# A relational graph layer on one core: gathered edge rows in plain f32 against weighted one-hot tables

## The chip, the cores and the metric

The kernel runs on one core of one Trainium2 chip. Its time is the device time of one execution, in microseconds (us). The kernel before took 3181.22 us, the median of three executions (3174.54 to 3181.66).

The engines are TensorE (PE; its weight loads have a row of their own, PEld), VectorE (DVE), ScalarE (ACT), GpSimd (POOL) and SyncE (SP), which issues most transfers. Each runs its own instructions in order and waits for the others at semaphores.

## The reference

`x` is 12500 nodes by 256 channels; there are 200000 edges, sorted by destination, each with a source, one of 8 types and a weight. Cut to what matters:

```
xn  = layernorm(x)
msg = xn[src] * edge_weight
h   = segment_sum(msg, type*N + dst) / max(count, 1)      # mean over (type, dst)
gnn = einsum('rnc,rco->no', h, weight) + xn @ root + bias
mix = linear attention of xn (8 heads, elu+1 features, one global k-v sum) @ wo + bo
x   = x + gnn + mix
x   = x + mixture_of_experts(layernorm(x))                # router, 6 experts of 3 layers, best 2
```

## The kernel before

**First stage (phase A).** The products `xn @ weight[r]` are formed for all nodes and 8 types and written to a table `y_tab` of 100000 rows of 256 floats in device memory. A table `etab` holds for each edge the row of `y_tab` that it needs, its destination, and its coefficient (weight over count). An edge's message is then one row of `y_tab` times one coefficient. This stage is the same in both kernels.

**Second stage (phase C)** works through 25 groups of up to 512 nodes (4 tiles of 128; the last group has 2). For each tile of nodes, 17 tiles of 128 edges are gathered: GpSimd issues one indirect DMA for each tile of edges into `ring` (L1159). A group's 68 tiles of edges come in 12 portions of 6, 6 and 5, and `ring` holds 6 portions. The sum over destinations is a matmul: the weights are a table `sel` (edge by node, 1 where the edge ends in the node), the moving operand is the 128 x 256 tile of rows, and the result is added in the PSUM accumulator `acc` of that tile of nodes.

**Precision.** Every large product is made from fp32r operands split in two: a high part, and a low part that is the rest. For the edges the table is exact, so two matmuls do: `sel` x `row_hi` and `sel` x `row_lo`. ScalarE makes `row_hi = fp32r(row * coefficient)` (L1216), VectorE makes `row_lo = row * coefficient - row_hi` (L1394) and the tables, one instruction for a portion (L1388), from a ramp that lies in PSUM. `sel` and `row_hi` have two buffers, `row_lo` six.

**Order within a loop pass i** (24 passes i = 0 to 23, then a last short one for the last 2 tiles). While the dense layers of group i run, the portions of group i+1 are put between them on TensorE. TensorE's order in a pass is: `queries` and `root` of group i+1; `turn` (8 transposes of the normalised group i, which wait for VectorE's layer norm, `xn_c`); portions 0 and 1 (`aggregate`, L1709); router and first layer of expert 0; portion 2; then for each expert e the second layer of e, a portion if `BEHIND_H2` names one, the first layer of e+1, the portion that `AHEAD_W3` names, and the third layer of e; at the end `close_sum`, 8 products in plain f32 into the same accumulators (L1718). All split products are recorded at one helper line, L1655. The results of the dense layers go to five PSUM banks in turn; ScalarE and VectorE split each first or second layer's result (L1230, L1231, then L1473), and VectorE adds each third layer's result to `y` (L1540). ScalarE and VectorE have the edge work written in between these: `high` on ScalarE, `one_hot` and `low_rows` on VectorE.

Group 0's portions run ahead of the loop, together with 36 key and value products (L1655 with `xk`, L1810), in the stretch that is called the middle here.

Of the kernel before, what the change touches and what calls it, by code (L numbers as in the profile page):

```python
# [16 lines left out]
NT = P  # L17
# [19 lines left out]
SLOTS, BUFS = 6, 2  # L37
# [4 lines left out]
BEHIND_H2 = {2: 5, 3: 7, 4: 9}  # L42

# [9 lines left out]
def gps_layer(nc, x, src, dst, etype, ew, g_w, g_root, g_b, wq, bq, wk, bk, wv, bv, wo, bo,  # L53
# [21 lines left out]
    with whole:  # L75
# [800 lines left out]
        with pc:  # L876
# [47 lines left out]
            gate_t = rq[0:8, 1, :]  # L924
            with ExitStack() as px:
                ring = sbuf(px, "ring", [P, SLOTS, PT, C])
# [93 lines left out]
            hi_ready, lo_ready, portion_used = (sem(n) for n in ("hi_ready", "lo_ready", "portion_used"))  # L1020
# [23 lines left out]

            def between(e):
                return BEHIND_H2.get(e, AHEAD_W3.get(e, PARTS))
# [148 lines left out]
            def _(act):  # L1195
# [13 lines left out]
                def high(n, p, first=0, end=PT):  # L1209

                    if first == 0:
                        act.wait_ge(tab_in[n % 2], 16 * SUB * (n // 2 + 1))
                        act.wait_ge(rows_in[p % SLOTS], 16 * gathers(n, p))
                        act.wait_ge(portion_used, portions_before(n, p) - BUFS + 1)
                    for q, (t, k) in list(enumerate(tiles_of_portion(p)))[first:end]:
                        last = act.activation(row_hi[:, p % BUFS, q, :], ring[:, p % SLOTS, q, :],  # L1216
                                              ACT.Copy, scale=tab[:, n % 2, t, k, 2:3])
                    if end == PT:
                        last.then_inc(hi_ready, 1)

                def iteration(i, plan):
# [18 lines left out]
                    if more:  # L1240
                        high(i + 1, 2)
# [4 lines left out]
                    if more:  # L1246
                        high(i + 1, 3)
                    act.wait_ge(d_ready, i + 1)
                    act.activation(ex[:, 0:T, :], lg[:, 0:T, :], ACT.Exp).then_inc(ex_ready, 1)
                    for e in range(EXPERTS):  # L1250
                        for m in range(KC):
                            hidden("h2", e, m)
                            if more and e in BEHIND_H2 and AHEAD_W3[e] < parts(i + 1):
                                high(i + 1, AHEAD_W3[e], 3 * m, 3 * m + 3)
# [8 lines left out]
                        if more and between(e + 1) < parts(i + 1):  # L1263
                            high(i + 1, between(e + 1))
                    if more:
                        if i + 2 < SUPER:
                            for p in range(2):
                                high(i + 2, p)
# [16 lines left out]
                for p in range(PARTS):  # L1285
                    if p < LATER:
                        for j in range(SUB):
                            key_parts(SUB * p + j)
                            if p and j < 2:
                                high(0, p - 1, 3 * j, 3 * j + 3)  # L1290
                    else:
                        if p == LATER:
                            high(0, p - 1)
                        high(0, p)
# [13 lines left out]
                for p in range(2):  # L1308
                    high(1, p)
# [5 lines left out]
            def _(dve):  # L1315
# [29 lines left out]
                dve.tensor_copy(ramp[:, 0:P], iota_w[:, :])  # L1345
                dve.drain()
# [53 lines left out]
                def prepare(n, p):  # L1400
                    one_hot(n, p)
                    low_rows(n, p)
# [479 lines left out]
```

## Time and profile before

| | |
|---|---|
| timed, median of 3 | 3181.22 us |
| profiled execution, span | 3900.9 us |
| TensorE busy, of the span | 3132.7 us |
| VectorE busy | 2360.3 us |
| ScalarE busy | 2004.5 us |
| GpSimd busy | 1638.6 us |
| mean granted TensorE clock | 0.894 of 2.4 GHz |

The profiled execution is one execution with the profiler on; its span is 3900.9 us, 720 us above the timed median. Both numbers are needed to read this case: durations and orders come from the profiled one, the result is a timed one. A matmul is written with two records, one of PEld and one of PE; a matmul in plain f32 has two of each. Because matmuls overlap, the distance from one start to the next, and not the duration, is what one costs in a row of them.

### The profile page before, as it was taken

How to read it: one execution, taken by the hardware profiler on the slowest of the kernel's cores; microseconds unless marked ns; L12 is line 12 of the kernel's file. 1: busy time of each engine (PE TensorE's matmuls, PEld its weight loads, DVE VectorE, ACT ScalarE, POOL GpSimd, SP SyncE). 2: the span in 40 equal slices, each digit the busy share in tenths (PEclk: the TensorE clock that was granted, in tenths of full speed). 3: DMA queues.
4: the chain of work that ended last, by engine and by line, in shares of the span. 5: the costliest groups of instructions: out<-in, count | busy, mean ns of one | idle time of the engine just before them, and what ended most of it. 6: DMA issues, size and time to landing. Idle time of an engine off the chain costs nothing.

```text
span 3900.9 us, 48061 instructions
## 1 busy us (share of the span) xinstructions
PE 3132.7 (80%) x16807; PEld 2709.1 (69%) x16808; DVE 2360.3 (61%) x5405; ACT 2004.5 (51%) x3996; POOL 1638.6 (42%) x1696
## 2 busy tenths in 40 slices
PE   6999999766878778777777777787787778787788
PEld 5888887656767767666666667676676667677677
DVE  4497552246666667566666656666565666666675
ACT  3555555334555555454555555555555455545564
POOL 0000000145555555554555555554545455555540
PEclk9999999888888888888889888888888889898899
DMA  6665555543233333233323333233323333233320
GB/s 242 250 259 196 210 210 212 224 144 112 84 93 95 99 96 94 82 94 91 90 77 96 95 92 89 85 97 89 92 83 91 90 93 91 79 97 93 100 67 11
DMA packets 179841, 456.72 MB, mean 117 GB/s; under 512 B 46604, under 2 KB 104918, under 8 KB 159405
## 3 DMA queue, kind: packets, MB, share of 16 engines
q0 software_dynamic: 80352, 219.14, 19.5%
q1 hardware_dynamic: 97074, 232.64, 16.5%
q8 instruction: 134, 2.20, 0.2%
q10 hardware_dynamic: 2172, 1.85, 0.1%
q14 instruction: 109, 0.89, 0.1%
HBM read 296.01 MB, written 158.29 MB: 116 GB/s over the span
## 4 chain that ended last, share of the span: by engine, by line
PE 41%; another core or an unknown queue 12%; DVE 10%; ACT 10%; issue 7%; DVEq 1%; DMA 0%; SPq 0%; ACTq 0%
PE bank L1655 27%; PE acc L1709 7%; DVE row_lo L1394 4%; ACT row_hi L1216 4%; ACT bank L1231 3%; ACT h_hi L1230 2%; PE acc L1718 1%; PE bank L1793 1%; PE bank L1682 1%; PE bank L1691 1%; PE acc L1655 1%; DVE y L1540 1%; DVE h_lo L1473 1%; DVE sel L1388 1%
## 5 line engine op out<-in xcount | busy, mean ns | idle before, releaser
L1159 POOL DMA_INDIRECT ring<-y_tab,tab x1666 | 1624.1, 975 | 1401.6 <-PE acc L1709 869.9
L1230 ACT ACTIVATE h_hi<-bank,bias_t 128x512 fp32r<-128x512 f32 (+1 forms) x600 | 408.9, 682 | 1078.1 <-remote 565.1
L1709 PE MATMUL acc<-row_hi,sel 128*128 128x256 f32 x1666 | 501.6, 329 | 446.5 <-DVE row_lo L1394 255.5
L1709 PEld LDWEIGHTS acc<-row_hi,sel 128*128 128x128 f32 x1666 | 369.9, 222 | 508.3 <-DVE row_lo L1394 291.1
L1216 ACT ACTIVATE row_hi<-ring,tab 128x256 fp32r<-128x256 f32 x1666 | 704.1, 510 | 31.4 <-PE acc L1709 19.4
L1394 DVE SCALAR_TENSOR_TENSOR row_lo<-ring,tab,row_hi 128x256 fp32r<-128x256 f32 x1666 | 685.1, 479 | 48.9 <-ACT row_hi L1216 34.4
L1473 DVE TENSOR_TENSOR h_lo<-bank,h_hi 128x512 fp32r<-128x512 f32 (+1 forms) x600 | 392.6, 676 | 447.2 <-ACT bank L1231 360.5
L790 PE MATMUL yb<-wr_hi,xhl 128*128 128x512 f32 x1568 | 510.9, 398 | 31.5 <-ACT yst L351 25.4
L1655 PE MATMUL bank<-ew_hi,h_hi 128*128 128x256 f32 x1176 | 384.2, 327 | 179.0 <-DVE h_lo L1473 177.7
L1709 PE MATMUL acc<-row_lo,sel 128*128 128x256 f32 x1666 | 480.9, 315 | 13.4 <-issue 13.2
L1540 DVE SCALAR_TENSOR_TENSOR y<-bank,gate,y 128x256 f32<-128x256 f32 x490 | 213.0, 479 | 349.7 <-PE bank L1655 227.7
L1655 PEld LDWEIGHTS bank<-ew_hi,h_hi 128*128 128x128 f32 x1176 | 268.7, 229 | 198.9 <-DVE h_lo L1473 196.3
L351 ACT ACTIVATE yst<-yb 128x512 f32<-128x512 f32 x392 | 230.5, 595 | 321.3 <-PE yb L790 283.6
L1231 ACT ACTIVATE bank<-bank,bias_t 128x512 f32<-128x512 f32 (+1 forms) x600 | 392.1, 654 | 0.0
L1709 PEld LDWEIGHTS acc<-row_lo,sel 128*128 128x128 f32 x1666 | 374.3, 225 | 11.3 <-issue 8.2
L1655 PE MATMUL bank<-ew_lo,h_hi 128*128 128x256 f32 x1176 | 371.2, 316 | 0.0
L790 PEld LDWEIGHTS yb<-wr_hi,xhl 128*128 128x128 f32 x1568 | 296.2, 189 | 104.6 <-ACT yst L351 26.3
L1655 PE MATMUL bank<-ew_hi,h_lo 128*128 128x256 f32 x1176 | 367.4, 312 | 0.0
L790 PE MATMUL yb<-wr_lo,xhl 128*128 128x512 f32 x784 | 311.5, 397 | 0.0
L1388 DVE TENSOR_TENSOR sel<-ramp,rel_w 128x768 fp32r<-128x768 f32 (+1 forms) x294 | 265.6, 903 | 6.4 <-issue 4.9
L1655 PEld LDWEIGHTS bank<-ew_lo,h_hi 128*128 128x128 f32 x1176 | 267.6, 228 | 0.1
L1655 PEld LDWEIGHTS bank<-ew_hi,h_lo 128*128 128x128 f32 x1176 | 264.9, 225 | 0.0
(272 smaller groups left out, 5219.7 us busy)
## 6 DMA issues: line engine op xcount, KB each, us to landing
y_tab<-yst SPq DMA_DIRECT2D x97, 1024.0 KB, 3.9
ring<-y_tab,tab POOLq DMA_INDIRECT x1666
xt_tab<-xhl SPq DMA_DIRECT2D x25, 1024.0 KB, 3.9
xc<-xt_tab SPq DMA_DIRECT2D x25, 1024.0 KB
x<-x_tab SPq DMA_DIRECT2D x49, 256.0 KB
xs<-in_x SPq DMA_DIRECT2D x24, 512.0 KB, 6.0
x_tab<-xs SPq DMA_DIRECT2D x24, 512.0 KB, 5.0
out<-y SPq DMA_DIRECT2D x24, 512.0 KB
```

What stands on the lines that cost most here:

```text
L351: act.activation(yst[:, h, 2 * b:2 * b + 2, :], yb[(YB * u + b) % 3][:, :].rearrange("p (r n) -> p r n", r=2), ACT.Copy).then_inc(y_ev, 1)
L790: last = pe.matmul(out_ap, a, b, start=(i == 0), stop=(i == len(parts) - 1))
L1159: pool.indirect_dma_start(out=out_ap, out_offset=None, in_=y_tab[:, :], in_offset=bass.IndirectOffsetOnAxis(ap=idx_ap, axis=0)).then_inc(s ...
L1216: last = act.activation(row_hi[:, p % BUFS, q, :], ring[:, p % SLOTS, q, :], ACT.Copy, scale=tab[:, n % 2, t, k, 2:3])
L1230: act.activation(dest[:, m, 0:W], b[:, 0:W], ACT.Relu, bias=bias)
L1231: act.activation(b[:, 0:W], b[:, 0:W], ACT.Relu, bias=bias).then_inc(h_set, 1)
L1388: dve.tensor_tensor(sel[:, p % BUFS, 0:size, :], ramp[:, 0:P].unsqueeze(1).to_broadcast([P, size, NT]), rel_w[:, n % 2, t, k:k + size].uns ...
L1394: last = dve.scalar_tensor_tensor(out=row_lo[:, p % SLOTS, q, :], in0=ring[:, p % SLOTS, q, :], scalar=tab[:, n % 2, t, k, 2:3], in1=row_h ...
L1473: gone(dve.tensor_tensor(lo_[:, m, 0:W], bank[plan[kind, (e, m)][0]][:, 0:W], hi[:, m, 0:W].bitcast(F32), ALU.subtract))
L1540: last = dve.scalar_tensor_tensor(out=y[:, t, :], in0=b[:, (t % 2) * C:(t % 2 + 1) * C], scalar=gate[:, t, e:e + 1], in1=(y if e else x1)[ ...
L1655: last = pe.matmul(out_ap, a, b, start=(begin and i == 0), stop=(not more and i == len(parts) - 1), skip_group_check=more)
L1709: last = pe.matmul(sums(t), sel[:, p % BUFS, q, :], half, start=False, stop=False, skip_group_check=True)
```

## The change

ScalarE no longer makes `row_hi`, VectorE no longer makes `row_lo`, and both buffers are gone. VectorE writes, for each tile of edges, a table that holds the edge's coefficient in place of the 1: one tensor_scalar of 128 x 128, (ramp is_equal destination) times coefficient, from SBUF to SBUF. TensorE multiplies this table with the gathered rows as they arrived, both in plain f32: one matmul as written for each tile of edges in place of two. TensorE waits for the rows and for the tables itself. `sel` has four buffers instead of two and is prepared further ahead. The PSUM bank that held the ramp becomes a sixth bank for the dense layers. Portion 0 stands ahead of the transposes instead of behind them. The gathers, the number of tiles and all dense work are the same.

```diff
-SLOTS, BUFS = 6, 2
+SLOTS, BUFS = 6, 4
+READY_AT = {0: (5,), 1: (6,), 2: (7, 8), 3: (9, 10), 4: (11,)}
...
-            row_lo = sbuf(pc, "row_lo", [P, SLOTS, PT, C], F32R)
-            row_hi = sbuf(pc, "row_hi", [P, BUFS, PT, C], F32R)
-            sel = sbuf(pc, "sel", [P, BUFS, PT, NT], F32R)
+            sel = sbuf(pc, "sel", [P, BUFS, PT, NT])
...
-            NBANK = 5
+            NBANK = 6
-            ramp = psum(pc, "ramp")
...
-                def high(n, p, first=0, end=PT):
-                    if first == 0:
-                        act.wait_ge(tab_in[n % 2], 16 * SUB * (n // 2 + 1))
-                        act.wait_ge(rows_in[p % SLOTS], 16 * gathers(n, p))
-                        act.wait_ge(portion_used, portions_before(n, p) - BUFS + 1)
-                    for q, (t, k) in list(enumerate(tiles_of_portion(p)))[first:end]:
-                        last = act.activation(row_hi[:, p % BUFS, q, :], ring[:, p % SLOTS, q, :],
-                                              ACT.Copy, scale=tab[:, n % 2, t, k, 2:3])
...
-                def one_hot(n, p):
+                def prepare(n, p):
+                    if p >= parts(n):
+                        return
                     dve.wait_ge(portion_used, portions_before(n, p) - BUFS + 1)
-                    (t, k), size = tiles_of_portion(p)[0], len(tiles_of_portion(p))
-                    dve.tensor_tensor(sel[:, p % BUFS, 0:size, :], ramp[:, 0:P].unsqueeze(1).to_broadcast([P, size, NT]),
-                                      rel_w[:, n % 2, t, k:k + size].unsqueeze(2).to_broadcast([P, size, NT]), ALU.is_equal)
-                def low_rows(n, p):
-                    dve.wait_ge(hi_ready, PARTS * n + p + 1)
                     for q, (t, k) in enumerate(tiles_of_portion(p)):
-                        last = dve.scalar_tensor_tensor(out=row_lo[:, p % SLOTS, q, :], in0=ring[:, p % SLOTS, q, :],
-                                                        scalar=tab[:, n % 2, t, k, 2:3],
-                                                        in1=row_hi[:, p % BUFS, q, :].bitcast(F32),
-                                                        op0=ALU.mult, op1=ALU.subtract)
-                    last.then_inc(lo_ready, 1)
+                        last = dve.tensor_scalar(sel[:, p % BUFS, q, :], iota_w[:, :], rel_w[:, n % 2, t, k:k + 1],
+                                                 tab[:, n % 2, t, k, 2:3], ALU.is_equal, ALU.mult)
+                    last.then_inc(sel_ready, 1)
...
                 def aggregate(n, p):
-                    pe.wait_ge(lo_ready, PARTS * n + p + 1)
+                    pe.wait_ge(sel_ready, PARTS * n + p + 1)
+                    pe.wait_ge(rows_in[p % SLOTS], 16 * gathers(n, p))
                     for q, (t, k) in enumerate(tiles_of_portion(p)):
-                        for half in (row_hi[:, p % BUFS, q, :], row_lo[:, p % SLOTS, q, :]):
-                            last = pe.matmul(sums(t), sel[:, p % BUFS, q, :], half, start=False, stop=False,
-                                             skip_group_check=True)
+                        last = pe.matmul(sums(t), sel[:, p % BUFS, q, :], ring[:, p % SLOTS, q, :], start=False, stop=False,
+                                         skip_group_check=True)
...
                         root(i, plan)
+                        aggregate(i + 1, 0)
                     turn(i, plan)
                     if more:
-                        aggregate(i + 1, 0)
                         aggregate(i + 1, 1)
```

TensorE at the start of a loop pass, before: behind `root` (the first two rows, into `acc`) come the transposes of the layer-normed group, and only then portions 0 and 1. The last two rows stand twelve times in turn, for the high and the low rows of 12 tiles of edges; the router's first products follow.

```order
L1655 MATMUL acc<-wqr_lo,xc 128x256
L1655 MATMUL acc<-wqr_hi,xc 128x256
L1701 MATMUL bank<-ident,xn_c 128x128 x8
L1709 MATMUL acc<-row_hi,sel 128x256
L1709 MATMUL acc<-row_lo,sel 128x256
```

The same place in the changed kernel, to the router's first products:

```order
L1592 MATMUL acc<-wqr_lo,xc 128x256
L1592 MATMUL acc<-wqr_hi,xc 128x256
L1648 MATMUL acc<-ring,sel 128x256 x6
L1638 MATMUL bank<-ident,xn_c 128x128 x8
L1648 MATMUL acc<-ring,sel 128x256 x6
L1592 MATMUL bank<-ft_hi,rw_hi 128x512
```

Portion 0 moved ahead of the transposes, portion 1 stayed behind them, and each counts 6 matmuls as written instead of 12.

VectorE from the second layer of expert 3 to its third layer, before. The first `h_lo` row belongs to the second layer's first half; `sel` and `row_lo` rows are edge work for the next portions.

```order
L1473 TENSOR_TENSOR h_lo<-bank,h_hi 128x512
L1388 TENSOR_TENSOR sel<-ramp,rel_w 128x640
L1473 TENSOR_TENSOR h_lo<-bank,h_hi 128x512
L1394 SCALAR_TENSOR_TENSOR row_lo<-ring,tab,row_hi 128x256 x5
L1473 TENSOR_TENSOR h_lo<-bank,h_hi 128x512 x2
L1388 TENSOR_TENSOR sel<-ramp,rel_w 128x768
L1540 SCALAR_TENSOR_TENSOR y<-bank,gate,y 128x256 x2
L1394 SCALAR_TENSOR_TENSOR row_lo<-ring,tab,row_hi 128x256 x6
L1540 SCALAR_TENSOR_TENSOR y<-bank,gate,y 128x256 x2
```

The same place in the changed kernel, with the rows of expert 4's layers behind it:

```order
L1421 TENSOR_TENSOR h_lo<-bank,h_hi 128x512 x4
L1350 TENSOR_SCALAR sel<-iota_w,rel_w,tab 128x128 x12
L1480 SCALAR_TENSOR_TENSOR y<-bank,gate,y 128x256 x4
L1341 TENSOR_SCALAR rel_w<-tab 128x17 x4
L1421 TENSOR_TENSOR h_lo<-bank,h_hi 128x512 x4
```

The edge work that stood between the splits of the dense layers is gone; what is left of it is one run of 12 short instructions ahead of the additions to `y`.

## Rows read from the trace of the kernel before

**Rows 1.** The page: span, and busy time, share and instructions of each engine.

```profile
span 3900.9 us, 48061 instructions
PE 3132.7 (80%) x16807; PEld 2709.1 (69%) x16808; DVE 2360.3 (61%) x5405; ACT 2004.5 (51%) x3996; POOL 1638.6 (42%) x1696
```

**Rows 2.** Busy time by stretch: one pass, A, middle, 23 loop passes, rest.

```profile
core 0: us, PE busy (x) PEld busy (x) DVE busy (x) ACT busy (x) POOL busy (x), PEclk, DMA share, GB/s
1186.36:1305.05 118.69, 94.09 (x535) 82.80 (x534) 77.56 (x187) 63.94 (x129) 65.20 (x67) 0.88 0.31 93
0.00:744.00 744.00, 701.19 (x3238) 572.12 (x3239) 400.85 (x735) 391.62 (x725) 14.23 (x29) 0.98 0.60 222
744.00:933.80 189.80, 122.24 (x587) 99.19 (x586) 95.05 (x188) 68.68 (x158) 98.75 (x95) 0.80 0.49 163
933.80:3776.00 2842.20, 2197.16 (x12283) 1937.71 (x12282) 1787.18 (x4279) 1476.43 (x2974) 1525.58 (x1572) 0.87 0.31 91
3776.00:3901.00 125.00, 112.08 (x704) 100.07 (x702) 77.17 (x204) 67.77 (x139) 0.00 (x0) 0.95 0.04 14
```

**Rows 3.** Waits by who waited for whom, whole span: us in total, times, longest.

```profile
ACT h_hi L1230 <- remote: 565.1, 79, 11.1
...
PE acc L1709 <- DVE row_lo L1394: 255.5, 81, 8.9
...
PE acc L1709 <- issue: 203.1, 71, 7.1
...
PE bank L1655 <- DVE h_lo L1473: 179.6, 36, 10.5
```

**Rows 4.** Timeline of one late hand-over: start, us, instruction, [idle before <-releaser].

```profile
1208.78 0.39 PE L1655 MATMUL bank<-ft_hi,ew_lo 128*128 128x512 f32 x1
...
1218.54 0.69 ACT L1230 ACTIVATE h_hi<-bank,bias_t 128x512 fp32r<-128x512 f32 x1 [8.95 <-remote]
```

**Rows 5.** Timeline of TensorE: matmuls in a row, by kind.

```profile
1183.10 3.62 PE L1718 MATMUL acc<-kw_sb,qf 128*128 128x256 f32 x16
...
1192.20 1.07 PE L1701 MATMUL bank<-ident,xn_c 128*128 128x128 f32 x8
...
1195.78 0.28 PE L1709 MATMUL acc<-row_hi,sel 128*128 128x256 f32 x1
1195.90 0.28 PE L1709 MATMUL acc<-row_lo,sel 128*128 128x256 f32 x1
...
1198.64 0.39 PE L1655 MATMUL bank<-ft_lo,ew_hi 128*128 128x512 f32 x1
1198.87 0.39 PE L1655 MATMUL bank<-ft_hi,ew_lo 128*128 128x512 f32 x1
```

**Rows 6.** Groups by line and shape, whole span: busy, mean ns, idle before.

```profile
L1718 PE MATMUL acc<-kw_sb,qf 128*128 128x256 f32 x400 | 91.2, 379 | 2.4 <-issue 2.4
```

**Rows 7.** Groups of one pass, VectorE and ScalarE: busy us, mean ns, idle before.

```profile
L1394 DVE SCALAR_TENSOR_TENSOR row_lo<-ring,tab,row_hi 128x256 fp32r<-128x256 f32 x68 | 27.9, 480 | 2.4 <-ACT row_hi L1216 1.7 <-issue 0.5
...
L1388 DVE TENSOR_TENSOR sel<-ramp,rel_w 128x768 fp32r<-128x768 f32 x8 | 7.6, 947 | 0.1
L1388 DVE TENSOR_TENSOR sel<-ramp,rel_w 128x640 fp32r<-128x640 f32 x4 | 3.3, 816 | 0.0
...
L1216 ACT ACTIVATE row_hi<-ring,tab 128x256 fp32r<-128x256 f32 x68 | 28.7, 510 | 0.1
```

**Rows 8.** Timeline of VectorE's tensor_scalar in runs of four, 128x128 and 128x256.

```profile
107.97 0.86 DVE L480 TENSOR_SCALAR diag<-ident,vmm 128x128 f32<-128x128 f32 x4
...
1190.67 1.38 DVE L1494 TENSOR_SCALAR xn_c<-x,mv_c,rstd_c 128x256 f32<-128x256 f32 x4
```

**Rows 9.** Timeline: two waits of TensorE for VectorE.

```profile
1180.16 0.39 PE L1655 MATMUL bank<-ew_hi,h_hi 128*128 128x256 f32 x1 [1.67 <-DVE h_lo L1473]
...
1196.97 0.47 PE L1655 MATMUL bank<-ft_hi,rw_hi 128*128 128x512 f32 x1 [0.80 <-DVE ft_lo L1503]
```

**Rows 10.** Timeline of GpSimd: one of a row of gathers.

```profile
1204.01 0.94 POOL L1159 DMA_INDIRECT ring<-y_tab,tab  x1 [0.30 <-issue]
```

More of the change, by code:

```diff
@@ L1042, in portions_before @@
                 return PARTS * n + p + SLOTS
-            def between(e):
-                return BEHIND_H2.get(e, AHEAD_W3.get(e, PARTS))
             def tiles_of_portion(p):
@@ L1262, in iteration @@
                             gone(act.activation(gate_t[:, 0:W], take(i, plan, "gt", 0)[0:8, 0:W], ACT.Copy))
[L1263 to L1268, printed above, removed]
                 act.dma_start(wo_sb[:, :, :], wo.rearrange("(k p) n -> p k n", p=P)).then_inc(small_c, 16)
@@ L1463, in iteration, with low @@
                     more = plan is LOOP
-                    def low(kind, e, table=None):
+                    def low(kind, e):
                         if e == EXPERTS:
@@ L1469, in low @@
                         for m in range(KC):
-                            if m and table is not None:
-                                one_hot(i + 1, table)
                             dve.wait_ge(h_set, nth_hidden(i, kind, e, m) + 1)
@@ L1487, in iteration @@
                     last.then_inc(var_c, 1)
-                    if more:
-                        one_hot(i + 1, 1)
                     dve.wait_ge(std_c, i + 1)
@@ L1509, in iteration @@
                     if more:
-                        prepare(i + 1, 3)
+                        prepare(i + 1, 4)
                     for e in range(EXPERTS):
-                        second = AHEAD_W3[e] if more and e in BEHIND_H2 and AHEAD_W3[e] < parts(i + 1) else None
-                        low("h2", e, second)
-                        if second is not None:
-                            low_rows(i + 1, second)
+                        low("h2", e)
                         if e == 0:
@@ L1524, in iteration @@
                             attention(i, plan)
-                        if more and e == EXPERTS - 1:
-                            if i + 2 < SUPER:
-                                prepare(i + 2, 0)
-                        coming = between(e + 1) if more and between(e + 1) < parts(i + 1) else None
-                        if coming is not None:
-                            one_hot(i + 1, coming)
+                        for p in READY_AT.get(e, ()) if more else ():
+                            prepare(i + 1, p)
+                        if e == EXPERTS - 1 and i + 2 < SUPER:
+                            prepare(i + 2, 0)
+                            prepare(i + 2, 1)
                         if e == 0:
@@ L1591, in _ @@
                             if p and j == 0:
-                                one_hot(0, p - 1)
-                            if p and j == 2:
-                                low_rows(0, p - 1)
+                                prepare(0, p - 1)
                     else:
@@ L1763, in iteration @@
                         hidden("h2", e)
-                        if more and BEHIND_H2.get(e, PARTS) < parts(i + 1):
+                        if more and e in BEHIND_H2:
                             aggregate(i + 1, BEHIND_H2[e])
@@ L1768, in iteration @@
                             denominators(i, plan)
-                        if more and AHEAD_W3[e] < parts(i + 1):
+                        if more:
                             aggregate(i + 1, AHEAD_W3[e])
```

36 lines of the change are left out of this document (7 added, 29 removed).

## The prediction

> **What bounds the kernel now.** I read the page first for its shares, then the stretches, then TensorE's timeline for what a matmul costs, then the waits.
>
> The page gives TensorE the largest share, 80% [rows 1], and the stretches show that the edges matter in one part only: phase A is the same in both kernels; the middle (190 us) holds the edges of group 0; 23 loop passes take 2842.2 us, 123.6 each; the last 125 us hold pass 23 and the short pass [rows 2]. So the argument is about a loop pass.
>
> The profiled execution is 720 us longer than the timed median of 3181 us, and that has to be placed before any sum. In phase A TensorE is busy for 701 of 744 us, so little of the excess can lie there. In the loop there are waits that no work explains. In [rows 4] TensorE has recorded the first layers up to 1209.2, but ScalarE, which had nothing to do but take a bank, starts at 1218.54 and is released by nothing that the profile names. Such waits sum to 565 us on ScalarE, and TensorE stands still for 203 us more with no releaser [rows 3]: 768 us together, about the 720. I take them for a burden of the profiled execution. That is an inference, since no timed run has a trace.
>
> What a timed pass takes follows from the median. Outside the loop and its tail are 933.8 us profiled; I take 29 us off for waits of the same kind and slow clock in the middle (granted 0.80 [rows 2]), and get 905. The short last pass is about 38 of the last 125 us. Pass 23 prepares only 34 tiles of edges, so it has 8 us less of matmuls. So 24 passes b give 3181 = 905 + 24b - 8 + 38, **b = 93.6 us**.
>
> What TensorE alone needs comes from distances between starts at full clock (2.4 GHz) [rows 5]: a split product of 512 columns costs 0.231 (1198.64 to 1198.87; in other places 0.227 to 0.234), one of 256 columns 0.119 (1195.78 to 1195.90), and a record of a plain f32 product of 256 columns 0.216: 16 of them in 3.62 us, the last lasting 0.379 [rows 6], so (3.62 - 0.38)/15. The code gives the counts of a pass, 534, which the stretch of one pass bears out with 535 records [rows 2]. 162 of 512 columns make 37.4 us. 304 of 256 columns make 36.2, of which the edges' 136 are 16.2. 24 plain f32 records make 5.2. 44 small ones at 0.11 (8 transposes in 1.07 us, the last lasting 0.28) make 4.8. That is **83.6 us**. A timed pass then has 93.6 - 83.6 = 10 us in which TensorE waits: TensorE is nearly the bound now, and the rest are hand-overs from VectorE and ScalarE (row_lo, h_lo) [rows 3].
>
> **The change, part by part, for one loop pass.**
>
> *Fewer but dearer matmuls.* 68 tiles of edges had two matmuls at 0.119, 0.238 us a tile. They get one as written, in plain f32 with the same 128 x 256 shape as `close_sum`, whose 200 products as written show 400 records [rows 6]. So a tile costs two records at 0.216, 0.432 us. The difference is 0.194 x 68 = **+13.2 us** on TensorE. Nothing can hide work on the engine that is itself the bound. TensorE's own work becomes 83.6 - 16.2 + 29.4 = 96.8 us: above the whole timed pass of today. The weight load of f32 lasts less than the 0.216 and overlaps, as it does in `close_sum`. I see no cheaper end for this price, since the row is of the same shape and kind.
>
> *ScalarE.* 68 `row_hi` of 28.7 us go [rows 7]. ScalarE falls from 63.9 to 35 us. This is worth something only through TensorE's waits, since ScalarE takes the dense results out of the banks and the edge work stood between them.
>
> *VectorE.* 27.9 + 7.6 + 3.3 = 38.8 us go [rows 7]. 68 tensor_scalars of 128 x 128 come. Four `diag` of that shape take 0.86 us, 0.215 each; the upper bound is the 128 x 256 form with two column operands, 1.38/4 = 0.345 [rows 8]; below the first I see no reason to go. I take the first, which has the shape: 14.6 us (at most 23.5). VectorE falls from 77.6 to 53 us (at most 62). Both lie beside TensorE's 96.8. Where the tables are made, in one run ahead of the additions to `y`, 12 of them take 2.6 us (at most 4.1); TensorE meanwhile has two portions (5.2 us) and a first layer (2.8 us) ahead of the third layer, and the six banks leave room. So this costs nothing; without that cover it would be 2 us for each of three experts, +6.
>
> *The new waits of TensorE* are for rows and tables. GpSimd starts a gather every 1.24 us (0.94 and 0.30 idle [rows 10]), 68 of them in 84.6 us a pass, 12 us under TensorE's work, with six portions of slack in `ring`. The tables are made four portions ahead. Both are ready.
>
> *Portion 0 ahead of the transposes.* From the end of `close_sum` the layer norm takes about 5.8 us to `xn_c`, and `queries` (2.8) and `root` (2.9) just cover it today. Portion 0 adds 2.6 us of cover. Behind the transposes portion 1 now lasts 2.6 us, where two portions lasted 2.9, so the 0.80 us wait for `ft_lo` stays [rows 9].
>
> *What remains of the 10 us of waiting.* The waits for `row_lo` go by construction. Those for `h_lo` shrink: between the end of a second layer and its use TensorE has 5.4 us of work and needs two steps of ScalarE and one of VectorE, some 2.1 us, no longer held up by edge work. I keep the 0.80 and the 1.67 us behind expert 5 [rows 9], where no first layer follows: **2.5 us**. The pass is 96.8 + 2.5 = 99.3 us, 5.7 more than 93.6.
>
> *The middle.* TensorE has +13 us for 68 tiles. But this stretch is bound by VectorE's hand-overs, and in each of nine portions 3.3 us of VectorE (`sel` 0.9, six `row_lo` of 0.4) become 1.2, -18. Net -5.
>
> *Sum.* 23 x 5.7 = 131. Pass 23 has 34 tiles: +6.6 of work, less 7.5 of waits, -1. Middle -5. 3181 + 125 = 3306; I say **3310**.
>
> Against the profiled span the same sum holds for the work (+13.2 a pass); what the span itself will be depends on the unexplained waits, which I can't forecast: if they stay, about 3900.9 + 125.
>
> **Two rules of the skill.** GpSimd's gathers start every 1.24 us beside VectorE's work today [rows 10]. The Trainium skill (SBUF — State Buffer, "SBUF: two separate sides") says that while VectorE runs an instruction that reads through both its ports, GpSimd can't write descriptors, and f32 tensor_scalar from SBUF to SBUF would be one. An estimate by it adds at most the 14.6 us of the new tables to 84.6, 99.2, just level with the 99.3 of a pass, so the sum would stand; with the upper bound of the tables it would be 108 and GpSimd the bound, which is the third rival. No row here shows a gather held up by such an instruction. The second is about the price of a matmul. The rows show 0.231 and 0.119 us at full clock [rows 5]. The Trainium skill (TensorE: Matmul & The Clock Gate, "Back-to-back issue gap") gives columns/2.4 GHz + 2.5 ns, so 0.216 and 0.109: the plain f32 record agrees with it, the split products don't. What that would do is the second rival.
>
> **Rivals.**
>
> *Nothing is given back.* The 10 us of waiting might be of the dense layers' own hand-overs and stay. Then every pass takes the full +13.2: 3181 + 23 x 13.2 + 6.6 + 13 = 3504. For it speaks that `h_lo` is among the waits [rows 3]; against it that `row_lo` is the larger one, and that a longer run of edge matmuls covers the others. Chance 0.10.
>
> *TensorE has more room than it seems* (the other side). If the fp32r products run in timed executions at 0.216 and 0.109, the place is every product of every stage. TensorE's need today is then 83.6 - 162 x 0.015 - 304 x 0.010 = 78.1, after the change 96.8 - 162 x 0.015 - 168 x 0.010 = 92.7; phase A with its 2724 products of 512 columns (98 tiles x 24 and 62 x 6) is 48 us shorter, so b = 95.6. A pass becomes 95.2, and the whole 3181 - 9 - 8 - 5 = 3159. It decides as soon as a timed pass of today exceeds TensorE's new need plus its waits. Against it: in the same pass the plain f32 records stand 0.216 apart [rows 5], so the profiler doesn't keep TensorE from that distance, and what makes the split products longer is theirs. Chance 0.08.
>
> *GpSimd becomes the bound.* If the new tensor_scalars hold up the gathers by more than 14.7 us a pass, portions arrive late. At 102 to 104 us a pass: 3370 to 3415. For it: 68 new instructions between VectorE's and GpSimd's common memory; against it: GpSimd is busy for 65 of 119 us of a pass today [rows 2], though VectorE reads two operands from SBUF in every `row_lo`. Chance 0.06.
>
> *The price of plain f32 isn't paid*, because a table times rows is treated otherwise than `close_sum`. Nothing in the trace speaks for it. Chance 0.02, at 3000 to 3100.
>
> **How the numbers follow.** The forecast, TensorE at its own work with 1 to 6 us of waits a pass, has 0.74. Its ends: b is 92.4 if nothing is taken off the 934 us and 95.1 if 64 us are, which moves the result by -35 to +30; waits of 1 or 6 us move it by -36 to +84. Together 3240 to 3425. With the GpSimd rival in it, and a little of the room of the other two, the range is **3225 to 3430**. A measurement here tells 0.3% (10 us) from no change. Slower by more than that: forecast, nothing given back, GpSimd, and part of the second rival, 0.88; within it 0.04; faster 0.08.
>
> **What would show it.** The records of `aggregate` should be 3332, 0.38 us each, 0.216 apart at full clock, 29.4 us a pass. ScalarE should have some 35 us a pass, VectorE some 53, with the tables 0.2 us apart. TensorE's clock should be full for longer, and its waits for VectorE nearly gone but for `ft_lo` and expert 5's `h_lo`. I am wrong if the records of `aggregate` are cheaper, if TensorE waits for `rows_in`, or if `h_lo` waits stay as long as they are.

## The result, and the profile after

The changed kernel takes 3283.09 us (median of 4 runs, 3275.71 to 3284.55), the kernel before 3181.44 us (4 runs, 3174.54 to 3186.5): ratio 1.0318, 95% interval 1.03 to 1.0337, so 3% slower. The forecast was 3310 us, within 3225 to 3430.

The page of the changed kernel begins like this (span, then busy time, share of the span and instructions of each engine), and answers to [rows 1]:

```profile
span 3280.2 us, 46098 instructions
## 1 busy us (share of the span) xinstructions
PE 3192.2 (97%) x16807; PEld 2743.8 (84%) x16808; DVE 1908.8 (58%) x5110; ACT 1359.2 (41%) x2330; POOL 1605.3 (49%) x1696
```

TensorE is busy for 97% of the span, with the same 16807 records; the 80% of [rows 1] are a share of the long span, and in the kernel before profiled again it is 93%. VectorE lost 451 us and ScalarE 645. This profiled execution is as long as the timed ones. That of the kernel before, at 3900.9 us, was not, so the two spans can't be subtracted. For that reason the kernel before was run and profiled again (`b0_again`). Its span is 3183.0 us, its waits hold no "remote" row on ScalarE, and all comparisons by stretch below use it.

The stretches of the kernel before, profiled again (columns as in [rows 2]): the middle, the 23 full passes of the loop, the rest.

```profile
744.00:904.00 160.00, 112.08 (x596) 93.33 (x595) 94.76 (x188) 72.13 (x166) 99.86 (x94) 0.88 0.57 192
904.00:3056.30 2152.30, 2020.93 (x12284) 1780.34 (x12283) 1777.84 (x4280) 1479.31 (x2968) 1544.49 (x1573) 0.98 0.41 120
3056.30:3183.00 126.70, 114.49 (x704) 102.66 (x702) 77.13 (x204) 68.03 (x139) 1.48 (x2) 0.93 0.05 16
```

The same stretches of the changed kernel:

```profile
0.00:744.00 744.00, 699.84 (x3233) 571.17 (x3235) 400.67 (x735) 391.47 (x725) 14.23 (x29) 0.98 0.60 222
744.00:897.20 153.20, 121.33 (x591) 99.11 (x590) 76.32 (x181) 41.00 (x86) 96.86 (x93) 0.91 0.59 200
897.20:3150.80 2253.60, 2253.60 (x12285) 1968.99 (x12283) 1364.26 (x4005) 867.41 (x1403) 1492.25 (x1572) 0.99 0.39 115
3150.80:3280.00 129.20, 117.39 (x704) 104.56 (x702) 67.55 (x191) 59.34 (x117) 1.99 (x3) 0.96 0.06 16
```

The loop is where the time went. 2152.3 us for 23 passes are 93.58 us each before; 2253.6 are 97.98 after, +4.40 a pass and +101.3 in all. The middle gives 6.8 us back, the rest costs 2.7 (the second span ends 0.2 us after the last stretch). Together 97.2 us, the difference of the two spans. In the loop TensorE is busy for 2253.60 of 2253.60 us: the profile shows no wait of it any more. Before, it was idle for 131.4 us of 2152.3.

TensorE at the start of a pass of the changed kernel (timeline: start, us, instruction; [rows 5] answers to it):

```profile
1000.11 0.28 PE L1592 MATMUL acc<-wqr_hi,xc 128*128 128x256 f32 x1
1000.23 2.75 PE L1648 MATMUL acc<-ring,sel 128*128 128x256 f32 x12
1002.81 1.04 PE L1638 MATMUL bank<-ident,xn_c 128*128 128x128 f32 x8
1003.69 2.76 PE L1648 MATMUL acc<-ring,sel 128*128 128x256 f32 x12
1006.09 0.58 PE L1592 MATMUL bank<-ft_hi,rw_hi 128*128 128x512 f32 x1
```

Portion 0 is 12 records in 2.75 us, the last lasting 0.38: (2.75 - 0.38)/11 = 0.215 us from start to start. The first product with `ft_hi` has no idle time before it, where 0.80 us stood in [rows 9].

The costliest groups by line, from the page of the changed kernel (busy, mean ns of one, idle before and who ended it):

```profile
L1212 ACT ACTIVATE h_hi<-bank,bias_t 128x512 fp32r<-128x512 f32 (+1 forms) x600 | 408.3, 681 | 962.3 <-PE bank L1592 935.8
L1421 DVE TENSOR_TENSOR h_lo<-bank,h_hi 128x512 fp32r<-128x512 f32 (+1 forms) x600 | 405.9, 680 | 678.3 <-ACT bank L1213 678.2
L1648 PE MATMUL acc<-ring,sel 128*128 128x256 f32 x3332 | 772.0, 380 | 4.0 <-DVE sel L1350 3.9
L1350 DVE TENSOR_SCALAR sel<-iota_w,rel_w,tab 128x128 f32<-128x128 f32 x1666 | 449.6, 357 | 2.7 <-issue 0.4
```

The direction of the waits has turned. ScalarE now stands idle for 936 us until TensorE fills a bank, VectorE for 678 us behind ScalarE, and TensorE waited for tables for 3.9 us in the whole run.

### The profile page after: what moved, and what is told of

It is laid out like the page before. It is cut to its first block, busy times and chain, and to the rows that moved or that the text cites. A ratio compares the mean times of both kernels' runs of the same rounds, so it can differ in the third digit from the quotient of the medians.

```text
span 3280.2 us, 46098 instructions
## 1 busy us (share of the span) xinstructions
PE 3192.2 (97%) x16807; PEld 2743.8 (84%) x16808; DVE 1908.8 (58%) x5110; ACT 1359.2 (41%) x2330; POOL 1605.3 (49%) x1696
## 4 chain that ended last, share of the span: by engine, by line
PE 74%; DVE 1%; DMA 1%; ACT 1%; issue 0%; SPq 0%; DVEq 0%; ACTq 0%
PE bank L1592 42%; PE acc L1648 22%; PE acc L1657 3%; PE acc L1592 2%; PE bank L1732 1%; PE bank L1619 1%; PE bank L1628 1%; PE bank L1638 1%; PE bank L1698 1%; PE bank L1749 0%; DMA xk<-xt_tab 0%; PE bank L1714 0%; DVE zv L1503 0%; DVE sel L1350 0%; ACT ew_hi L1271 0%
## 5 line engine op out<-in xcount | busy, mean ns | idle before, releaser
L1648 PE MATMUL acc<-ring,sel 128*128 128x256 f32 x3332 | 772.0, 380 | 4.0 <-DVE sel L1350 3.9
L1648 PEld LDWEIGHTS acc<-ring,sel 128*128 128x128 f32 x3332 | 628.3, 191 | 94.8 <-DVE sel L1350 4.5
L1350 DVE TENSOR_SCALAR sel<-iota_w,rel_w,tab 128x128 f32<-128x128 f32 x1666 | 449.6, 357 | 2.7 <-issue 0.4
L1592 PE MATMUL bank<-ew_lo,h_hi 128*128 128x256 f32 x1176 | 328.3, 279 | 0.0
L1592 PE MATMUL bank<-h_hi,ew_hi 128*128 128x512 f32 (+1 forms) x600 | 246.3, 411 | 1.3 <-DVE h_lo L1421 1.3
L1592 PE MATMUL bank<-ft_hi,ew_hi 128*128 128x512 f32 (+1 forms) x600 | 247.2, 412 | 0.0
L1592 PE MATMUL bank<-h_lo,ew_hi 128*128 128x512 f32 (+1 forms) x600 | 241.5, 402 | 0.0
L1592 PE MATMUL bank<-h_hi,ew_lo 128*128 128x512 f32 (+1 forms) x600 | 241.4, 402 | 0.0
L1592 PE MATMUL bank<-ft_hi,ew_lo 128*128 128x512 f32 (+1 forms) x600 | 233.7, 390 | 0.0
L1592 PEld LDWEIGHTS bank<-ew_hi,h_hi 128*128 128x128 f32 x1176 | 220.5, 188 | 13.9 <-DVE h_lo L1421 11.4
```

The costliest lines, as they stand in the source:

```text
L1350: last = dve.tensor_scalar(sel[:, p % BUFS, q, :], iota_w[:, :], rel_w[:, n % 2, t, k:k + 1], tab[:, n % 2, t, k, 2:3], ALU.is_equal, ALU. ...
L1592: last = pe.matmul(out_ap, a, b, start=(begin and i == 0), stop=(not more and i == len(parts) - 1), skip_group_check=more)
L1648: last = pe.matmul(sums(t), sel[:, p % BUFS, q, :], ring[:, p % SLOTS, q, :], start=False, stop=False, skip_group_check=True)
```

## The experiments

The theory: a pass of the changed kernel is TensorE's own work, and what the kernel before lost beside its work was VectorE's low rows arriving late, which the change gives back. The rivals: the price of the matmuls is something else; the waits of before belonged to the dense layers; the sixth bank or the place of portion 0 matters. First come cuts into the kernel before, then cuts into the changed one, then mixtures.

### The kernel before, unchanged: `b0_again`

> The kernel before, unchanged, profiled once more. Theory: the 565 us that ScalarE and the 203 us that TensorE waited with no releaser belong to that one profiled execution and not to the timed ones. Then this execution either has them again (span near 3900 us, timed near 3181) or shows a span near 3180 us with 24 passes of about 93.6 us and some 10 us of TensorE's waits in each. Rival (the waits are the kernel's own): every profile of it would show them, and its timed runs could not be at 3181.

Measured: 3184.47 us, profiled span 3183.0 us. TensorE's waits in this second profile, first of the whole span, then of the loop alone (who waited for whom: us in total, times, longest):

```profile
PE acc L1709 <- DVE row_lo L1394: 117.8, 84, 6.4
```

```profile
PE acc L1709 <- DVE row_lo L1394: 98.3, 75, 2.1
PE bank L1655 <- DVE ft_lo L1503: 18.2, 23, 0.8
PE bank L1655 <- DVE h_lo L1473: 10.3, 23, 0.5
```

The unexplained waits of [rows 3] (565 us of ScalarE, 203 of TensorE) are gone, and so are the 720 us: they belonged to one profiled execution. What stays is the wait for `row_lo`: 98.3 of the 131.4 us that TensorE is idle in the loop, 4.3 a pass. `ft_lo` holds 18.2 and `h_lo` 10.3.

### The low matmuls left out: `b1_high_only`

The kernel before without the second matmul of each tile. The low rows are still made, and not used.

```diff
-for half in (row_hi[...], row_lo[...]):
+for half in (row_hi[...],):
```

> The kernel before with TensorE's 68 low matmuls of a pass left out, the low rows still made: TensorE needs 75.5 us a pass instead of 83.6, ScalarE and VectorE do all their work. Left out: the low part of the edge sums. If TensorE is the bound and its waits are a fixed addition: 3181 - 24 x 8.1 = 2990 us. If VectorE and ScalarE set the pass through their order, the time hardly moves: 3120 to 3181 us. I expect between, near 3060 us, since both are close to the bound.

Measured: 3146.55 us, ratio 0.9898 (0.9879 to 0.9917). One pass (columns as in [rows 2]), and its wait for low rows:

```profile
1085.20:1175.40 90.20, 79.32 (x468) 69.06 (x467) 77.17 (x187) 63.86 (x129) 65.21 (x68) 0.98 0.41 123
```

```profile
PE acc L1709 <- DVE row_lo L1394: 189.3, 107, 6.4
```

68 matmuls at 0.119, 8.1 us of TensorE's work a pass, are gone, and the kernel is only 34 us shorter, 1.4 a pass; I had expected about 120. The pass shown is one of the shortest; the 23 take 92.2 us on average. Part of the difference is the clock, granted at 0.958 on average against 0.971 in `b0_again`, but even the shortest passes are only 2 us under a full-clock pass of the kernel before, which also takes 92.2 (in `b3_six_banks`). The wait for `row_lo` grew from 117.8 to 189.3 us. So before, taking work off TensorE was worth little: VectorE's low rows set the pass.

### The low rows not made: `b2_no_low`, and the high rows neither: `b4_no_edge_work`

In the first, VectorE makes the low rows of one tile in each portion, and both matmuls of a tile read the high rows. In the second, ScalarE too makes one tile in each portion. The sums over edges are left incomplete in both. TensorE has all its matmuls.

```diff
-for q, (t, k) in enumerate(tiles_of_portion(p)):
+for q, (t, k) in list(enumerate(tiles_of_portion(p)))[0:1]:
     last = dve.scalar_tensor_tensor(out=row_lo[...
```

> The kernel before with VectorE making the low rows of only the first tile of each portion and TensorE multiplying the high rows twice: TensorE's work is the same 83.6 us a pass, VectorE has some 22 us less. Left out: the low part of the edge sums. Theory (the 10 us of waits of a timed pass come from edge work that stands between the dense layers' hand-overs, most of it VectorE's): 5 to 9 us a pass less, 2960 to 3060 us. Rival (the dense layers' own hand-overs cause them): 3150 to 3181 us.

> As the one without low rows, and ScalarE makes the high rows of only the first tile of each portion: TensorE's 83.6 us a pass stand against nearly no edge work elsewhere but the one-hot tables. Left out: most of the edges' rows (one tile's rows stand for the portion's). Theory: a pass of 84 to 86 us (GpSimd's 84.6 us of gathers is then as long as TensorE's work), 3181 - 24 x 8.5 = about 2975 us. Rival (dense hand-overs): above 3120 us.

Measured: 2989.51 us, ratio 0.94 (0.9383 to 0.9417), and 2977.1 us, ratio 0.9362 (0.9345 to 0.9379). One pass of the first:

```profile
1147.00:1232.70 85.70, 84.68 (x537) 75.62 (x535) 56.28 (x130) 64.21 (x129) 64.97 (x69) 1.00 0.45 131
```

VectorE has 21 us less in a pass (77.2 to 56.3), and the pass falls by 8 us, from 93.6 to 85.6. ScalarE's high rows are worth 12 us more in all. So nearly all the waits of the kernel before come from VectorE's low rows, and hardly any from ScalarE or from the dense layers' own hand-overs. The fall can't be much larger: TensorE is busy for 84.68 of the 85.70 us, and what is left is above all one wait of 0.9 us a pass for expert 5's `h_lo`. In the whole run:

```profile
PE bank L1655 <- DVE h_lo L1473: 25.0, 27, 2.1
```

The wait for `ft_lo`, 20.2 us in 25 times before, is gone with VectorE's low rows too: 1.2 us, once.

### Half the columns: `a1_half_columns`

The changed kernel, with each edge matmul over 128 of the 256 columns, so half of each sum is left out.

```diff
-pe.matmul(sums(t), sel[...], ring[:, p % SLOTS, q, :], ...
+pe.matmul(sums(t)[:, 0:C // 2], sel[...], ring[:, p % SLOTS, q, 0:C // 2], ...
```

> The changed kernel with each edge matmul over 128 of the 256 columns. Left out: half of the edge sums. Theory (a record of plain f32 costs its columns twice over at full clock, 0.216 us for 256 and 0.11 for 128, and TensorE is the bound): 68 x 0.216 = 14.7 us a pass less on TensorE, 82 us; then GpSimd's gathers, 68 x 1.24 = 84.6 us, are the bound. 84.6 to 86 us a pass instead of 98: 3283 - 24 x 12.5 = about 2985 us. Rival (the price doesn't hang on the columns): near 3283 us.

Measured: 2979.8 us, ratio 0.9369 (0.9348 to 0.939). The pass is 85.0 us where it was 98.0. TensorE's busy time falls from 3192.2 to 2846.9 us. Two waits have come back, though ScalarE and VectorE do the same as in the changed kernel:

```profile
PE bank L1592 <- DVE h_lo L1421: 27.0, 27, 2.1
...
PE bank L1592 <- DVE ft_lo L1449: 10.7, 25, 1.2
```

TensorE's work falls by 14.6 us a pass (68 x 0.215), from 97.3 to 82.7 at full clock, and the pass to 85.0, and what remains beside the work is above all those waits, 0.9 and 0.4 us a pass. In the changed kernel they stand at 4.8 us (4 times) and 1.2 (once), none of it in the loop. So the longer edge matmuls are what covers them there: with expert 5, TensorE has only portion 11, five tiles, between the second layer and the third.

### Tables and rows as fp32r: `a4_fp32r`

The changed kernel with the tables written, and the rows read, as fp32r: one record a tile in place of two, and the sums over edges only at fp32r's precision.

```diff
-sel = sbuf(pc, "sel", [P, BUFS, PT, NT])
+sel = sbuf(pc, "sel", [P, BUFS, PT, NT], F32R)
-... ring[:, p % SLOTS, q, :], start=False ...
+... ring[:, p % SLOTS, q, :].bitcast(F32R), start=False ...
```

> The changed kernel with the tables written as fp32r and the gathered rows read as fp32r: one split-free fp32r matmul for each tile of edges, so the edge sums carry the precision of fp32r only. TensorE needs 96.8 - 29.4 + 8.1 = 75.5 us a pass, below GpSimd's 84.6. Theory: 84.6 to 87 us a pass, 2950 to 3010 us; the whole loss of the change is the price of plain f32 on TensorE, and all the relief of ScalarE and VectorE is kept. Rival (VectorE's tables at 0.27 us each or the order limit it): above 3100 us.

Measured: 2962.41 us, ratio 0.9311 (0.9291 to 0.9331). Who ended the idle time of GpSimd's gathers, in this kernel:

```profile
L1153 POOL DMA_INDIRECT ring<-y_tab,tab x1666 | 1596.9, 959 | 523.7 <-issue 502.7 <-PE acc L1648 14.7 <-DMA tab<-etab 6.3
```

```profile
PE acc L1648 <- DMA ring<-y_tab,tab: 65.1, 32, 3.8
```

The type is the whole price: with fp32r the change would have been 7% faster than the kernel before, but its sums have only fp32r's precision. The run also shows the next bound. With the gaps left out TensorE's work is some 76 us in a pass at full clock (78.4 where the lower clock falls in it), yet a pass takes 84.8 us on average and 85.5 in the middle of the run: GpSimd hardly waits for a free slot any more (14.7 us in the whole run, against 326 in the changed kernel), and TensorE waits for gathered rows.

### The bank and the place of portion 0: `a2_five_banks`, `a3_portion0_behind`, `b3_six_banks`

The first is the changed kernel with five banks, the second the changed kernel with portion 0 behind the transposes as before, the third the kernel before with six banks.

```diff
-NBANK = 6
+NBANK = 5
```

```diff
-    aggregate(i + 1, 0)
 turn(i, plan)
 if more:
+    aggregate(i + 1, 0)
```

> The changed kernel with five banks for the dense layers instead of six. Theory: the banks are worth nothing here, since TensorE has work ahead of each hand-over: 3280 to 3290 us. Rival (the sixth bank is what emptied the waits): 1 us or more a pass, above 3305 us.

> The changed kernel with portion 0 behind the transposes again. Queries and root last 5.7 us, the layer norm 5.8 from the end of the closing products. Theory: 0 to 0.8 us a pass more ahead of the transposes, nothing behind them: 3283 to 3303 us.

> The kernel before with a sixth accumulator bank (the position row read from SBUF instead of from the eighth bank) and nothing else. If the changed kernel's loss is the price of its edge matmuls alone, the bank is worth nothing: 3176 to 3188 us, ratio 0.998 to 1.002. If banks held TensorE before, it would be 20 us or more faster.

Measured: 3280.63 us, ratio 1.0313 (1.029 to 1.0337); 3285.71 us, ratio 1.0332 (1.031 to 1.0355); 3183.63 us, ratio 1.0008 (0.9996 to 1.002). Neither bank nor place is worth anything that can be measured, in either kernel.

### More buffers, and the edge work further ahead: `c3_three_bufs`, `c2_lookahead3`

If VectorE's place in the order were the cause, rather than its amount of work, the kernel before could be saved by preparing further ahead. The first has three buffers in place of two and four ring slots in place of six (the memory doesn't hold more). The second adds six banks and writes each portion's high rows, table and low rows one portion earlier.

```diff
-SLOTS, BUFS = 6, 2
+SLOTS, BUFS = 4, 3
```

> The kernel before with three buffers of high rows and tables in place of two, and four ring slots in place of six; no line is moved. Theory (low rows late because VectorE reaches them late in its own order, by its amount of work and the place in the code): a third buffer alone changes little, 3165 to 3190 us. Rival (VectorE or ScalarE waits for a buffer that TensorE has not yet given back, and that makes the low rows late): TensorE's waits for low rows fall by half or more and the time goes to 3080 to 3130 us.

> The kernel before, full computation, with three buffers and four ring slots, six banks, and ScalarE's high rows and VectorE's tables and low rows each written one portion earlier than before (the order of the changed kernel). TensorE's own work stays 83.6 us a pass. If the waits for low rows come from the place of VectorE's work, the pass falls to 87 to 90 us and the time to 905 + 24 x 88.5 + 30 = 3060 us (3020 to 3110). If VectorE's amount of work (77 us a pass) holds TensorE wherever it stands, it stays at 3150 to 3190 us.

Measured: 3182.55 us, ratio 1.0015 (1.0 to 1.003), and 3394.63 us, ratio 1.0674 (1.0645 to 1.0702). The buffers alone do nothing. The second is a miss: 335 us above the 3060 of the first theory and 205 above the upper end of the other. Its waits:

```profile
ACT row_hi L1217 <- issue: 459.2, 167, 6.8
...
PE bank L1643 <- DVE h_lo L1468: 296.9, 74, 9.3
...
PE acc L1697 <- DVE row_lo L1391: 19.2, 10, 6.4
```

TensorE's wait for low rows did fall, from 117.8 to 19.2 us. In its place it waits 296.9 us for `h_lo`. The timeline of GpSimd, ScalarE, VectorE and TensorE around one of these waits (the first row is the last gather of the portion whose high rows come next):

```profile
2056.23 1.30 POOL L1160 DMA_INDIRECT ring<-y_tab,tab  x1 [0.30 <-issue]
...
2059.45 1.30 ACT L1217 ACTIVATE row_hi<-ring,tab 128x256 fp32r<-128x256 f32 x3 [3.16 <-issue]
2060.66 0.67 ACT L1231 ACTIVATE h_hi<-bank,bias_t 128x512 fp32r<-128x512 f32 x1
...
2061.90 0.69 DVE L1468 TENSOR_TENSOR h_lo<-bank,h_hi 128x512 fp32r<-128x512 f32 x1 [2.22 <-ACT bank L1232]
...
2062.65 0.39 PE L1643 MATMUL bank<-ew_hi,h_hi 128*128 128x256 f32 x1 [3.49 <-DVE h_lo L1468]
```

ScalarE stands still for 3.16 us in front of a high row. The profile names only "issue", but the times show what it waits for. The last gather of that portion is issued at 2056.23, and the high row starts 3.2 us later; a gather lands 2.8 us after its issue (the median of the run). From 900 us on, 165 portions have such a wait of more than 0.5 us, 454 us together. Every one of them ends 2.7 to 4.5 us after the start of the portion's last gather, and in `b0_again`, where no portion waits, the distance is at least 16.8 us. So ScalarE waits for gathered rows: with four slots a gather can start only when TensorE has used the portion four before, and ScalarE now wants its rows a portion earlier. Behind the waiting high row on ScalarE stand the results of the dense layers, and they are late for TensorE. The run tells that edge work put ahead of its rows, and in front of dense work, costs more than it gives. It doesn't tell the place of VectorE's work from its amount, which it was meant to do; six slots don't fit beside three buffers and were not tried.

### Part of the portions each way: `d1_half_split`

The changed kernel computes everything on TensorE, the one before makes VectorE late. This one takes portions 3, 5, 7, 9 and 11 of every loop pass the old way, 28 of 68 tiles, and the rest the new way.

```diff
+def in_two(n, p):
+    return n >= 1 and p % 2 == 1 and p > 1
...
+if in_two(n, p):
+    for half in (row_hi[:, q, :], row_lo[:, p % SLOTS, q, :]):
+        last = pe.matmul(sums(t), sel_r[:, p % BUFS, q, :], half, ...
+    continue
```

> A mixture, full computation: the changed kernel, but in every pass of the loop portions 3, 5, 7, 9 and 11 (28 of the 68 tiles) go the way of the kernel before (one-hot table without the coefficient, high rows by ScalarE, low rows by VectorE, two matmuls), with three table buffers in place of four and one buffer of high rows. TensorE's own work falls by 28 x (0.432 - 0.238) = 5.4 us to 91.9 us a pass, VectorE's rises from 59 to about 70 us, still below the 77 of before. If VectorE's amount of edge work is what made the low rows late, half of it fits beside TensorE: pass 92 to 93.5, time 905 + 24 x 92.7 + 30 = 3160 us (3140 to 3175), a little faster than before. If every low row that TensorE waits for costs by its place (ScalarE's high rows, then VectorE's low rows, behind the waits of its own program order), the waits come back: 3190 to 3260 us.

Measured: 3174.0 us (10 runs), ratio 0.997 (0.9957 to 0.9982) to the kernel before. One pass:

```profile
2112.50:2205.20 92.70, 91.83 (x535) 81.16 (x534) 68.20 (x203) 48.81 (x89) 65.64 (x68) 1.00 0.41 121
```

TensorE's busy time is 91.8 us of the pass, as worked out ahead (91.9), VectorE's 68 (70 expected), and TensorE waits for 0.9, again for expert 5's `h_lo`, since portion 11 goes the old, shorter way here. With 28 tiles split, VectorE's edge work fits beside TensorE. The time is at the upper end of the 3140 to 3175 expected. It is the fastest of the kernels that compute everything at full precision, 0.3% under the kernel before, which is little but clear of the interval, and 3.3% under the changed one.

## Why the prediction was right

**The pass of today.** It was worked out from the timed median as 93.6 us; the second profile has 93.58. TensorE's own work was put at 83.6 us. In two full-clock passes of `b3_six_banks`, whose edge work is the same, the matmuls that follow each other without a gap take 83.7 and 83.8 us and the gaps, counted from start to start, 8.4 and 8.5. The rest of the 10 us are short stretches at the lower clock.

**The burden of the profiled execution.** That ScalarE's and TensorE's unexplained waits belong to it alone was an inference. `b0_again` shows it: without them the span is 3183.0 us.

**The price of a matmul.** Forecast 0.216 us from start to start, 3332 records, 0.38 us each. Measured 0.215 to 0.216, 3332, 0.380. A full-clock pass is 97.3 us of TensorE's work; the forecast was 96.8.

**The waits that remain.** This is the term that was mis-sized, and the reason why 3310 was 27 us too high. I kept 2.5 us a pass, 0.80 for `ft_lo` and 1.67 for expert 5's `h_lo`, and took the pass to 99.3. TensorE has no idle time in the loop. The two waits were read from the burdened execution [rows 9], and they counted as the dense layers' own. They went for two different reasons.

For `ft_lo` I looked at TensorE's cover only. In the kernel before, VectorE makes the six low rows of portion 1 between `xn_c` and `ft_lo`, as `b0_again` shows:

```profile
1282.94 1.39 DVE L1494 TENSOR_SCALAR xn_c<-x,mv_c,rstd_c 128x256 f32<-128x256 f32 x4
1284.24 2.46 DVE L1394 SCALAR_TENSOR_TENSOR row_lo<-ring,tab,row_hi 128x256 fp32r<-128x256 f32 x6
1286.62 1.28 DVE L1358 SCALAR_TENSOR_TENSOR qf<-eq,bank 128x512 f32<-128x512 f32 x2
1287.81 1.28 DVE L1503 TENSOR_TENSOR ft_lo<-bank,ft_hi 128x512 fp32r<-128x512 f32 x2
```

With them nearly gone in `b2_no_low` the wait is gone. In `a1_half_columns`, with half the cover, 0.4 us of it comes back. In `a3_portion0_behind` it is gone as well, so the place of portion 0 isn't needed for that. For `h_lo`, the second profile of the kernel before has only 0.5 us a pass (10.3 in 23), so most of the 1.67 belonged to the one execution. The rest doesn't come from VectorE's low rows: nearly without them (`b2_no_low`) 0.9 us a pass stands, and in `a1_half_columns`, which has none, too. It vanishes because portion 11, which alone stands between the second and third layers of expert 5, lasts 10 x 0.215 us in place of 10 x 0.12. I had priced these matmuls and not counted them as cover at this place. Two smaller errors went the other way. TensorE's own work is 0.5 us more than forecast, and 11 of the 23 full passes last 98.7 or 98.8 us in place of 97.3 for a short stretch at the lower clock, 0.7 us a pass on average, for which I had no term. With -2.5, +0.5 and +0.7 a pass is 98.0 us where I had 99.3, and 23 passes are 30 us less than forecast: the waits alone would have made it 57. That the total came out within 1% owes something to errors of opposite sign.

**The new tables.** 0.215 us each was too low. VectorE's timeline of the changed kernel has runs of 6 and 12:

```profile
1301.59 1.62 DVE L1350 TENSOR_SCALAR sel<-iota_w,rel_w,tab 128x128 f32<-128x128 f32 x6
...
1360.21 3.16 DVE L1350 TENSOR_SCALAR sel<-iota_w,rel_w,tab 128x128 f32<-128x128 f32 x12
```

With the last lasting 0.34 (the median of one), that is (1.62 - 0.34)/5 = 0.256 each, within the bounds of 0.215 and 0.345. VectorE has 59 us a pass where 53 were forecast, and ScalarE 37.7 where 35 were. With 38 us to spare on the one and 60 on the other, neither costs anything.

**The ends.** The middle gave 6.8 us (forecast 5). The last stretch cost 2.7 where I had a gain of 1: with the few waits of pass 23, its 6.6 us of added work outweighed them.

**The rivals.** *Nothing given back* (3504) is refuted: 8.8 of 13.2 us came back, and `b2_no_low` with `b1_high_only` shows that they were for the most part VectorE's low rows. *More room* (3159) is refuted: the split products of 256 columns stand 0.12 us apart in this undisturbed profile too, beside plain ones at 0.215. Its sum also had a slip: 2724 products at 0.015 are 41 us of phase A, not 48, which makes it about 3166. And the prediction's remark that the plain f32 record agrees with the rule it cites doesn't hold: that record has 256 columns and takes 0.216 us, twice the 0.109 that the prediction itself gives for 256. The forecast went by the rows and doesn't depend on it. *GpSimd as the bound* is refuted for this kernel:

```profile
L1153 POOL DMA_INDIRECT ring<-y_tab,tab x69 | 65.5, 949 | 33.0 <-issue 19.8 <-PE acc L1648 13.2
L1350 DVE TENSOR_SCALAR sel<-iota_w,rel_w,tab 128x128 f32<-128x128 f32 x68 | 18.4, 357 | 0.1
```

In this pass 68 two-operand tensor_scalars cost the gathers nothing that can be seen: they last 0.949 us on average, not longer than the 0.980 of a pass of `b0_again`, and GpSimd waits 13.2 us for TensorE. The Trainium skill (SBUF — State Buffer, "SBUF: two separate sides") says that GpSimd can't write descriptors while VectorE runs an instruction that uses both its ports. With these means the trace shows no delay by it. *The price of plain f32 isn't paid* is refuted by the 0.215.

## What to carry to other kernels

Sum each engine's own work and the waits of the bound engine apart. Here the edit moved work onto the engine that was nearly the bound. It paid the full price and won back at most that engine's waits: those that the removed work had caused, and one that the longer matmuls now cover; 13.2 against 8.8 us a pass. For each wait that a forecast keeps, ask what the other engine does just before its hand-over, and how long the waiting engine's own work in front of it will be after the change. When a pass is nearly balanced between two engines, moving part of the tiles one way and part the other can beat both pure forms, as the mixture did by a little. Profile twice before subtracting: one profiled execution can hold hundreds of microseconds that no timed run has.

## What was unexpected of the hardware

One profiled execution of the kernel before took 3900.9 us and the next 3183.0, of the same program, with timed runs between 3170 and 3192. The excess lay in waits, up to 11.1 us long, for which the profile names no work [rows 3, 4]. What caused them stays open.

A pass can hold one short stretch at the lower of TensorE's two clocks while TensorE has no idle time. The stretches of 4 us around one of them, in the changed kernel (columns as in [rows 2], granted clock after the busy times), and what TensorE did just before:

```profile
1036.00:1040.00 4.00, 4.00 (x26) 3.31 (x25) 2.70 (x6) 0.00 (x0) 3.05 (x4) 1.00 0.34 101
1040.00:1044.00 4.00, 4.00 (x12) 3.17 (x11) 1.12 (x2) 1.24 (x2) 1.67 (x2) 0.57 0.36 101
1044.00:1048.00 4.00, 4.00 (x19) 3.39 (x19) 0.69 (x1) 1.41 (x3) 1.03 (x2) 1.00 0.00 0
```

```profile
1037.71 1.99 PE L1732 MATMUL bank<-b_sb,rq 6*128 6x256 f32 x8
...
1041.22 0.63 PE L1592 MATMUL bank<-h_hi,ew_lo 128*128 128x512 f32 x1
1041.64 0.63 PE L1592 MATMUL bank<-h_hi,ew_hi 128*128 128x512 f32 x1
```

Products of 512 columns stand 0.42 us apart there (1041.22, 1041.64), and 0.23 elsewhere. It follows eight records that use 6 of the 128 rows, falls in the same place in 11 of 23 passes, and costs 1.5 us each time. What decides in which passes it happens stays open.

And gathers set a floor, which the forecast had as 84.6 us a pass and which `a4_fp32r` reaches. GpSimd starts one every 1.25 us, 68 x 1.25 = 85.0 us a pass. In `a4_fp32r` TensorE waits 65.1 us for gathered rows, and a pass takes 85.5 us in the middle of the run, though its work is shorter. `b2_no_low`, `b4_no_edge_work` and `a1_half_columns` have passes of 85.6, 85.3 and 85.0 us, and in them GpSimd waits for a free slot for less than 25 us in the whole run. But TensorE waits for no gathered row in any of the three, and its own matmuls take 83.7, 83.8 and 82.7 us of the pass, so there the two limits lie together and the floor isn't shown to be what holds. Whoever takes more than 8 us out of this pass has to shorten the gathers as well.
